# One transformer layer on eight cores: the second product two slots earlier, VectorE scaling two quads, value weights loaded by columns

## The reference, cut to what matters

```
x = x + attention(layernorm(x))          # causal, softmax(QK^T/8), no output projection
x = x + ffn(layernorm(x))
ffn: h = bit_linear(x, w1)               # activations rounded to 8 bits per token, weights to -1/0/1
     h = silu(depthwise_conv1d(h))       # 3 taps along the tokens, per hidden channel
     out = bit_linear(h, w2)             # again: scale of a token = 127 / max|h|, then round
```

## Time and profile before

| | us |
|---|---|
| median of 3 runs | 978.73 |
| profiled execution, whole | 977.3 |
| its span, slowest core (core 5) | 975.7 |
| other cores' spans | 969.7 to 975.1 |
| PE busy / DVE / ACT / POOL | 889.0 / 711.9 / 697.3 / 620.6 |

### The profile page before, as it was taken

The page is one execution under the profiler, slowest core; times in us unless marked ns, Lnnn a source line. Parts: engine busy times, 40 slices in busy tenths (PEclk is TensorE's granted clock), DMA queues, the critical chain, the costliest instruction groups (busy, mean ns, idle before and its releaser), DMA issues.

```text
span 975.7 us, 24133 instructions; the slowest of 8 cores (969.7 to 975.7 us)
## 1 busy us (share of the span) xinstructions
PE 889.0 (91%) x7516; PEld 538.3 (55%) x7516; DVE 711.9 (73%) x1173; ACT 697.3 (71%) x1108; POOL 620.6 (64%) x819
## 2 busy tenths in 40 slices
PE   1999899999999989998776699999999999999998
PEld 0454454555554545554654466666666666666443
DVE  2677665566666676669588988989899887877651
ACT  3554698889887888988988678678777777766300
POOL 2220648574655565545546978979799797978650
PEclk9999999999998999999989899999999999999999
...
GB/s 262 331 169 91 233 222 214 237 215 181 255 247 218 223 243 250 231 238 191 243 313 162 108 67 118 139 92 173 109 133 128 89 94 124 108 130 88 44 87 44
DMA packets 38891, 166.93 MB, mean 171 GB/s; under 512 B 4977, under 2 KB 5106, under 8 KB 30066
## 3 DMA queue, kind: packets, MB, share of 16 engines
...
...
## 4 chain that ended last, share of the span: by engine, by line
PE 75%; DVE 7%; ACT 6%; issue 6%; DMA 3%; POOL 2%; SPq 0%; DVEq 0%; ACTq 0%; POOLq 0%
PE psO L968 21%; PE psM L950 19%; PE psQK L748 11%; PE psS L806 7%; PE psPV L834 6%; PE psV L723 5%; ACT PT L1110 4%; DMA wvst<-wv 2%; DMA w1b<-t1scr 2%; PE psS L816 1%; DVE psD L1543 1%; DVE hs L1524 1%; POOL hs L667 1%; PE psK L748 1%; ACT hs L1159 1%
## 5 line engine op out<-in xcount | busy, mean ns | idle before, releaser
L1110 ACT ACTIVATE PT<-psS,nbias 128x1024 bf16<-128x1024 f32 (+1 forms) x320 | 299.9, 986 | 45.2 <-PE psS L806 27.2
L950 PE MATMUL psM<-xqT,w1b 128*128 128x258 bf16 x2048 | 242.9, 277 | 20.3 <-DVE hs L1524 16.2
L667 POOL TENSOR_TENSOR hs<-hs,tb 128x256 f32<-128x256 f32 x256 | 194.6, 784 | 68.2 <-DVE hs L1524 61.8
L950 PEld LDWEIGHTS psM<-xqT,w1b 128*128 128x128 fp8e4 x2048 | 200.7, 99 | 61.4 <-issue 24.3
L1159 ACT ACTIVATE hs<-psM,convb_s,convw_s 128x256 f32<-128x256 f32 x256 | 147.5, 576 | 86.2 <-PE psM L950 61.4
L676 POOL TENSOR_TENSOR hs<-hs,srow 128x256 f32<-128x256 f32 x240 | 178.5, 777 | 15.5 <-ACT srow L1177 15.4
L1524 DVE SCALAR_TENSOR_TENSOR hs<-psM,convw_s,hs 128x256 f32<-128x256 f32 x256 | 114.8, 476 | 23.7 <-ACT tb L1163 22.6
L1543 DVE TENSOR_REDUCE psD<-hs 128x256 f32<-128x1024 f32 x56 | 109.3, 1952 | 22.0 <-ACT hs L1170 22.0
L748 PE MATMUL psQK<-ln1T,wqkb 128*128 128x512 bf16 x480 | 124.0, 382 | 1.4 <-ACT qkO L1086 0.2
L1163 ACT ACTIVATE tb<-psM,convw_s 128x256 f32<-128x256 f32 x256 | 123.6, 483 | 0.0
L834 PEld LDWEIGHTS psPV<-vaug,PT 128*128 128x128 bf16 x2176 | 92.1, 98 | 50.8 <-issue 25.5
...
## 6 DMA issues: line engine op xcount, KB each, us to landing
...
```

The source lines that it names most:

```text
L667: e.tensor_tensor(hs_quad(q)[:, part], hs_quad(q)[:, part], tb_quad(q)[:, part], ALU.add).then_inc(g_add, 1)
L950: inst = e.matmul(psM[j][:, 0:GRP + 2], w1b[:, at:at + 128], xqT[:, x0:x0 + GRP + 2], start=(kc == 0), stop=(kc == 7))
L1110: e.activation(out=pt_unit(u).rearrange("p (h w) -> p h w", w=512)[:, :, 128 * j:512], in_=psS[u % 2][:].rearrange("p (h w) -> p h w", w=512)[
```

## The change

- **Second product.** `LAG = 14`: it starts in slot 14 (G=1, b=6) and runs 14 slots behind its quads. Within a group the order of its eight parts is now both first halves, then both second halves, for each 128 tokens. `add_out` moves from b = 2, 4, 6 and the next 0 to b = 1, 2, 5, 6; stores and `x1g` loads move accordingly.
- **VectorE scales two quads.** Quads 0 and 1 of each group (`OWN = 2`) are no longer scaled by POOL: DVE multiplies `hs` by `psNb` into a new 16-bit integer tile `hi` and copies that to `hqa`/`hqb` (`scale_round_h`). `SCALED` and `ROUNDED` move the rest up; quad 7 is rounded in slot 7 and no longer in slot 0 of the following group. The last group alternates: DVE scales quads 0, 1, 3, 5, 7, POOL 2, 4, 6. `turn_max` and `transpose_xq` wait until DVE has read `psNb`; `place_srow` waits for 6 quads a group.
- **Value weights by columns.** The four DMAs bring 512 rows x 512 columns each, column half 0 first; `values` works by column half, waits for the weights of its half alone, and does half 0 of tiles 0 to 2 ahead. Token tile 2 is loaded before the last two weight DMAs. POOL sets the ones of `vaug` in two parts.
- **Weight scales at pair ends.** The means move to slots 32 to 38 of head pairs 2 and 4; the guards of `norms` move from 6 and 10 to 7 and 11.
- **Loads of the first groups spread**, as the rows of SP below show.

```diff
@@ -244,6 +244,7 @@
         x1g = sb("x1g", [128, 2 * D], F32, esB)
+        hi = sb("hi", [128, QD], I16, esB)
         esT = ExitStack()
...
@@ -336,8 +353,11 @@
-        SCALED = {2: (0, 1), 3: (2,), 4: (3, 4), 5: (5,), 6: (6,), 7: (7,)}
-        ROUNDED = {3: (0, 1), 4: (2,), 5: (3, 4), 6: (5,), 7: (6,)}
+        SCALED = {2: (2,), 3: (3, 4), 4: (5,), 5: (6,), 6: (7,)}
+        ROUNDED = {3: (0, 1), 4: (2,), 5: (3, 4), 6: (5, 6), 7: (7,)}
+        OWN = 2
+        LAG = 14
...
@@ -368,8 +388,10 @@
                 e.dma_start(
-                    out=wv_quarter(n).rearrange("p (c d) -> p c d", d=D),
-                    in_=wv_h[256 * n:256 * (n + 1), :]
+                    out=wvst[:, 2048 * n:2048 * (n + 1)].rearrange(
+                        "p (c d) -> p c d", d=512),
+                    in_=wv_h[512 * (n % 2):512 * (n % 2 + 1),
+                             512 * (n // 2):512 * (n // 2 + 1)]
                     .rearrange("(c p) d -> p c d", p=128)
...
@@ -388,9 +410,9 @@
             load_x(1)
+            load_x(2)
             load_wv(2)
             load_wv(3)
-            load_x(2)
             load_x(3)
...
@@ -462,34 +484,34 @@
                         load_w1(q)
-                    if b == 1 and G >= 3:
-                        store_out(2 * (G - 3) + 1)
-                    if b == 2 and 3 <= G <= 9:
+                    if b == 3 and G >= 2:
+                        store_out(2 * (G - 2))
+                    if b == 4 and 2 <= G <= 8:
+                        load_x1g(2 * (G - 2) + 2)
+                    if b == 7 and G >= 2:
+                        store_out(2 * (G - 2) + 1)
+                    if b == 0 and 3 <= G <= 9:
                         load_x1g(2 * (G - 3) + 3)
-                    if b == 5 and G >= 2:
-                        store_out(2 * (G - 2))
-                    if b == 6 and 2 <= G <= 8:
-                        load_x1g(2 * (G - 2) + 2)
                     if b in (5, 6) and 9 <= 2 * G + b + 2 < NT:
...
                         e.wait_ge(d_x1s[2], 16)
-                        for st in range(5, 9):
-                            load_x1t(st)
-                    if G == 0 and b == 3:
+                        load_x1t(5)
+                        load_x1t(6)
+                    if G == 0 and b in (6, 7):
+                        load_x1t(b + 1)
+                    if G == 1 and b in (4, 5):
+                        load_x1g(b - 4)
+                    if 8 * G + b in (4, 6, 8, 10):
                         x1_spilled(e)
-                        load_x1g(0)
-                        load_x1g(1)
-                    if 5 <= 8 * G + b <= 8:
                         e.wait_ge(a_xqf, 2)
-                        q4 = 8 * G + b - 5
+                        q4 = 4 * G + b // 2 - 2
                         e.dma_start(
...
                         ).then_inc(d_w2, 16)
-            store_out(2 * NGRP - 1)
             e.wait_ge(d_out[0], 16 * NGRP)
...
@@ -593,19 +615,23 @@
                 e.wait_ge(d_wv[n], 16)
-                at = (2 * n + 1) * D
-                e.tensor_copy(Wvb[:, at:at + D],
-                              wvst[:, at:at + D]).then_inc(g_wv, 1)
+                e.tensor_copy(wvb_part(Wvb, n, 1),
+                              wv_quarter(n, 1).rearrange(
+                                  "p (c d) -> p c d", d=512)).then_inc(g_wv, 1)
+            ap = vaug[:].rearrange("p (s h w) -> p (s h) w", h=H, w=VW)
             cast_wv(0)
+            e.wait_ge(a_wv, 1)
+            e.wait_ge(g_wv, 1)
+            e.memset(ap[:, 0:3 * H, DH:DH + 1], 1.0).then_inc(g_vones, 1)
             cast_wv(1)
...
             e.wait_ge(g_wv, 4)
-            ap = vaug[:].rearrange("p (s h w) -> p (s h) w", h=H, w=VW)
-            e.memset(ap[:, :, DH:DH + 1], 1.0).then_inc(g_vones, 1)
+            e.memset(ap[:, 3 * H:, DH:DH + 1], 1.0).then_inc(g_vones, 1)
             cast_wqk(0, 0)
...
@@ -706,26 +729,25 @@
-            def values(st):
+            def values(st, nh):
+                n = HALVES.index((st, nh))
                 e.wait_ge(v_lnT, st + 1)
-                e.wait_ge(a_wv, 4)
-                e.wait_ge(g_wv, 4)
...
+                e.wait_ge(a_wv, 2 * (nh + 1))
+                e.wait_ge(g_wv, 2 * (nh + 1))
...
@@ -872,9 +895,15 @@
             turn_ln(1)
+            values(0, 0)
+            turn_ln(2)
+            values(1, 0)
+            values(2, 0)
             for st in range(NT):
-                values(st)
-                if st + 2 < NT:
+                if st >= 3:
+                    values(st, 0)
+                values(st, 1)
+                if 1 <= st and st + 2 < NT:
                     turn_ln(st + 2)
...
@@ -953,9 +982,11 @@
                     inst.then_inc(t_mm1, 1)
-            def second(g, b):
-                m, n, half = b // 4, (b // 2) % 2, b % 2
+            def second(k):
+                g, i = divmod(k, 8)
+                m, half, n = i // 4, i // 2 % 2, i % 2
                 o = 4 * g + 2 * m + n
...
@@ -998,10 +1030,11 @@
                         spread_scale(G - 1)
-                    if G == 2 and b == 0:
+                    k = 8 * G + b - LAG
+                    if k == 0:
                         e.wait_ge(d_w2, 64)
-                    if G >= 2:
-                        second(G - 2, b)
+                    if 0 <= k < 8 * NGRP:
+                        second(k)
                     if b == TAKEN[G > 0] + 2 and G < 7:
...
@@ -1119,10 +1153,10 @@
             norm1(1)
+            norm1(2)
             cast_wv(2)
             cast_wv(3)
-            norm1(2)
-            e.wait_ge(g_vones, 1)
+            e.wait_ge(g_vones, 2)
             for st in range(NT):
...
@@ -1438,12 +1472,20 @@
             place_ln(1)
+            place_ln(2)
             e.wait_ge(g_vones, 1)
+            place_v(0)
+            place_v(1)
+            place_v(2)
+            for st in range(3, 6):
+                moments(st)
+            e.wait_ge(g_vones, 2)
             for st in range(NT):
-                place_v(st)
-                if st + 3 < NT:
+                if st >= 3:
+                    place_v(st)
+                if st >= 3 and st + 3 < NT:
                     moments(st + 3)
-                if st + 2 < NT:
+                if st >= 1 and st + 2 < NT:
                     place_ln(st + 2)
...
@@ -1507,11 +1549,11 @@
                     weight_step(6 + STEPS.index(slot))
-                if (hp, s) in ((2, 8), (4, 8)):
+                if (hp, s) in ((2, 32), (4, 32)):
                     sum_columns(hp // 2 - 1)
-                if (hp, s) in ((2, 13), (4, 13)):
+                if (hp, s) in ((2, 35), (4, 35)):
                     mean_weight(hp // 2 - 1)
-                if (hp, s) in ((2, 17), (4, 17)):
+                if (hp, s) in ((2, 38), (4, 38)):
                     place_scale(hp // 2 - 1)
...
@@ -1567,27 +1609,36 @@
                                 ALU.mult).then_inc(v_deq, 1)
-            def scale_last(q):
-                e.wait_ge(a_srow, NGRP)
-                quad = hs_quad(q).rearrange("p (j s) -> p j s", s=GRP)
-                done(e.tensor_tensor(
-                    quad, quad, psNb[:, 256:512].unsqueeze(1).to_broadcast(
-                        [128, 4, GRP]), ALU.mult))
-            def round_h(q):
-                g, b = divmod(q, 8)
-                if q < LASTQ:
-                    e.wait_ge(g_mul, q + 1)
-                elif b % 2 == 0:
-                    e.wait_ge(g_mul, LASTQ + b // 2 + 1)
-                else:
-                    settled()
+            def place_h(q):
+                g = q // 8
                 if q == 0:
...
                     e.wait_ge(t_mm2, 4 * (g - 1))
-                e.tensor_scalar(hq_of(g)[:, QD * b:QD * (b + 1)], hs_quad(q),
+                return hq_of(g)[:, QD * (q % 8):QD * (q % 8 + 1)]
+            def scale_round_h(q):
+                g = q // 8
+                e.wait_ge(a_srow, g + 1)
+                if q >= 1:
+                    e.wait_ge(v_hq, q)
+                done(e.tensor_tensor(
+                    hi[:].rearrange("p (j s) -> p j s", s=GRP),
+                    hs_quad(q).rearrange("p (j s) -> p j s", s=GRP),
+                    psNb[:, 256:512].unsqueeze(1).to_broadcast(
+                        [128, 4, GRP]), ALU.mult))
+                settled()
+                e.tensor_copy(place_h(q), hi[:]).then_inc(v_hq, 1)
+            def round_h(q):
+                g, b = divmod(q, 8)
+                n = b // 2 if q >= LASTQ else b + 1 - OWN
+                e.wait_ge(g_mul, (8 - OWN) * g + n)
+                e.tensor_scalar(place_h(q), hs_quad(q),
                                 MAGIC, -MAGIC, ALU.add, ALU.add
...
@@ -1627,14 +1678,10 @@
                         taps(8 * G + b, (1,))
-                    if b == 0 and G >= 3:
-                        add_out(4 * (G - 3) + 3)
-                    if b in (2, 4, 6) and G >= 2:
-                        add_out(4 * (G - 2) + b // 2 - 1)
```

(23 more changed lines are left out.)

73 lines of the change are left out of this document (41 added, 32 removed).

## The result

The changed kernel runs at 1.0033 times the kernel before, 95% interval 1.0021 to 1.0045: 3.2 us slower, where 1.4 us faster was forecast. On 978.4 us (the median of before over 13 runs) that is 981.6 us, and the profiled execution took 981.93. (The median over all runs of the changed kernel, 999.34, holds runs in which the cores of one die had a lower clock; the ratios here leave such runs out.)

What follows compares the result with a forecast made beforehand. The prediction took PE to bound the feed-forward stage (busy 299.28 of 300 us), with vector engines setting the pace in its first 16 slots. Its terms, -3.1 - 6.9 + 7.6 + 0.7 + 0.3 = -1.4 us, gave 977.3 us, range 970.8 to 983.

Steps and rivals of the forecast that it cites:

- loads spread: Quad 5's w1 load goes ahead of two x1t tiles, ending nearly all of PE's 3.71 us wait: -3.1 us.
- two parts in slots 14 and 15: Two second-product parts leave the program's end and fill PE's waits in slots 14 to 17: -6.9 us.
- DVE's order in groups 2 to 5: DVE's scaling of two quads delays taps and the rounding of quads 3 and 7, so PE waits: +7.6 us.
- tail: Behind the last first product: waits for quad 7's rounding and two add_outs against earlier waits of 2.2 us: +0.7 us.
- first stage and rest: Program start: earlier value product against query weights requested later, up to 1.2 us lost there: +0.3 us.
- weight scales: A few short instructions at attention's pair ends, beside waits of that size: 0, within 0.5 us either way.
- B: DVE becomes the bound of four groups at quad 3's rounding, losing 15 us for 7.6: 984.7 us, chance 0.20.
- A: POOL's lighter load takes up the lateness, at most 1 us lost in all groups: 970.7 us, chance 0.18.
- C: Quad 5's w1 load still lands late, so the 3.1 us are missing: 980.4 us, chance 0.10.
- D: DVE's copy takes its lower bound of 0.34 us, 0.8 us less in each of four groups: 974.1 us, chance 0.14.

Runs made afterwards that it cites:

- loads_only: The kernel before with the spread loads of w1, tokens and w2 alone; ratio to before 0.9966, 3.3 us faster.
- new_start: The kernel before with the new first stage alone (value weights by columns, token tile 2 earlier); ratio to before 1.0020, 2.0 us slower.
- old_start: The changed kernel with the first stage of before; ratio to before 0.9998, 3.4 us below the changed kernel.
- scales_late: The kernel before with the weight scales computed at the pair ends; ratio to before 0.9994.
- rounds_first: The changed kernel with DVE's roundings in slots 5 and 7 ahead of the maximum; ratio to before 0.9951, 8.0 us below the changed kernel.
- tail_outs: The changed kernel with the third and fourth output of group 6 added one slot earlier; ratio to before 1.0001, 3.1 us below the changed kernel.
- ffn_only: The kernel before with the changed feed-forward stage alone, first stage and attention as before; ratio to before 1.0003.

## Why the prediction was wrong, term by term

| term | forecast | measured | from |
|---|---|---|---|
| loads spread | -3.1 | -3.3 (-4.7 to -2.1) | loads_only |
| two parts in slots 14 and 15 | -6.9 | hidden whole | traces |
| DVE's order in groups 2 to 5 | +7.6 | +5.7 | waits after slot 14 |
| tail | +0.7 | +3.5 | 1.91 + 2.15 - 2.2 + 1.68 |
| first stage and rest | +0.3 | +2.0 alone, +3.4 in the whole | new_start, old_start |
| weight scales | 0 | -0.6 (-2.0 to +0.9) | scales_late |

The step that failed first is "Start and the rest", put at +0.3 with 1.2 as the worst. I had the mechanism (the query weights are requested behind the third weight DMA, 1.6 us later) and a wrong size. On the mean of the eight cores the first request went out 1.15 us later than in before (20.96 for 19.81); the first load took no longer to its cast (10.5 us for 10.9), but the second took 1.3 us more (10.3 for 9.0), so that its cast came 2.0 us later. On the slowest core of each kernel (1 and 5) it was 4.5 us: the request 0.8 later, the loads 11.9 us for 9.7 and 10.6 for 9.1. Part of that is the choice of cores, since core 5 had one of the two fastest first loads of before's eight (9.7 to 11.9 us). Only 0.5 us of the lateness was slack (the casts of the earlier trace rows ended at 41.6, the projection began at 42.1). So the forecast took 1.6 us of lateness, let neither load grow and looked at one core; the second load grew, and the projection of the latest of the eight cores began 2.2 us later (46.29 for 44.09), 1.65 on the mean. Why the second load takes longer isn't shown: the DMAs are full in both kernels there (share 0.96 to 1.05 from 28 to 44 us).

The second is "The tail". Its first wait came as forecast, 1.91 us for my 2.2. "Two add_outs stand close before the parts that reuse their bank: 0.7 us" was the mis-sized step: the third addition stands behind four scalings and six roundings or copies in a row, and was done 2.15 us late. I had said only that the scaling of the last group ends in time, and had not placed the additions among it. And I had no price for the clock: 1.7 us on half of the cores, the slowest among them. In size the two errors are alike: 2.8 us here, 1.7 to 3.1 for the first stage.

Two steps went well. The loads gained what their rows promised. In slots 14 to 17 PE had two parts more, and yet reached the first part of slot 17 at 581.30 - 473.88 = 107.4 us after the start of the stage, where it took 579.00 - 467.35 = 111.7 before: 4.2 us sooner, for a forecast of 3.1 and a little. On the mean of the eight cores it is 2.5 us sooner (107.4 for 109.9), and loads_only, which has the spread loads without the two parts, reaches the same place after 107.6: the two parts cost nothing there.

The DVE term was near in size (5.7 for 7.6), and that was luck. Its wait for a tap in slot 5 was forecast at 1.1 us in four groups and measured 0.5 in all; its waits for quads 3 and 7 were forecast at 3.2 us and measured 5.2. The reason was wrong too. I took the waits as DVE's lack of time; rounds_first shows that the same work in another order leaves nearly none of them on core 0 and a part of them, at the taps, on the others. The prediction's rows held the order already: the roundings of the earlier trace rows stand behind a reduction. The copy took 0.63 us on the mean beside POOL (twelve from 600 to 900 us) for my 0.76, and 0.43 alone:

```profile
L1634 DVE CAST hqa<-hi 128x1024 f16<-128x1024 int16 x6 | 3.8, 636 | 1.0 <-DVE hi L1628 1.0
L1634 DVE CAST hqb<-hi 128x1024 f16<-128x1024 int16 x6 | 3.7, 624 | 0.9 <-DVE hi L1628 0.7
```
```profile
949.97 0.43 DVE L1634 CAST hqb<-hi 128x1024 f16<-128x1024 int16 x1 [0.17 <-DVE hi L1628]
```

(The last row is of tail_outs, with POOL idle.) By the Trainium skill, page "VectorE: DVE Perf Modes", section "The perf-mode tier table (the rule you actually need)", I had estimated 0.41 for a copy between 16-bit operands; the trace agrees, with 0.43.

With the measured terms the sum is -3.3 - 6.9 + 5.7 + 3.5 + 2.0 - 0.6 = +0.4 us, or +1.8 with 3.4 for the first stage, against +3.2 measured (2.1 to 4.4). The four terms of the feed-forward stage alone make -1.0, and ffn_only measured +0.3 (-1.2 to +1.8). What is left, 1.4 to 2.8 us, is no more than the intervals of the parts make together, each about 1.3 us either way; I can't assign it. Of the rivals, B was the right side by the wrong mechanism: the waits in the groups stayed under 2 us each. A and C are out: PE idled 6.1 us in 300, and the loads gained 3.3. D is out as a time; of its mechanism, a copy faster than I took it, 0.13 us came true, a third of the way to its bound of 0.34 us.
